# A wait on the landing of the output two windows back, in the scatter queue of a two-layer expert kernel

## The reference, cut to what matters

```python
# layer 1: one expert of 8 for each sequence
h = gelu(x @ Wi[expert] + bi[expert])          # 128 -> 512
o = h @ Wo[expert] + bo[expert]                # 512 -> 128
y = layernorm(o + x) * gamma[expert] + beta[expert]
# layer 2: FiLM on normalised y, then 2 experts of 8 for each token
h = film(time_norm(layernorm(y)))              # gains and shifts from the subject
probs = softmax(h @ router_w)
gates, idx = top_k(probs, 2); gates /= gates.sum()
out = y + sum_k gates[k] * (relu(h @ exp_w1[idx[k]] + exp_b1) @ exp_w2[idx[k]] + exp_b2)
```

## Time and profile before

| what | value |
|---|---|
| timed executions | 211.25, 212.04, 215.63 us; median 212.04 |
| span of the profiled execution | 215.0 us, first to last instruction |
| PE, PEld busy | 172.2 us (80%), 162.9 us (76%) |
| DVE, ACT, POOL busy | 128.2, 94.7, 112.1 us |
| outputs on POOL (L604) | 39, 962 ns each in the mean |

### The profile page before, as it was taken

One profiled execution on the slowest core, in us unless ns is written; L12 is line 12 of the kernel. 1 busy time (PEld: TensorE's weight loads), 2 busy tenths in 40 slices (PEclk: granted clock), 3 DMA queues, 4 the chain that ended last, 5 costly groups with the idle time before them and its releaser, 6 DMA issues.

```text
span 215.0 us, 5253 instructions
## 1 busy us (share of the span) xinstructions
PE 172.2 (80%) x1306; PEld 162.9 (76%) x1306; DVE 128.2 (60%) x635; ACT 94.7 (44%) x311; POOL 112.1 (52%) x168
## 2 busy tenths in 40 slices
PE   7999999999999996799926997436998999987000
PEld 6878999999998986689826896316998999976000
DVE  4515848999989998689725566003345455534154
ACT  2116444677484495537505462024454655552000
POOL 8860012556768987675762307773354454455300
PEclk9999999999999999999995999655799999999655
DMA  3999702999911684586741773211678667252294
GB/s 80 276 303 365 255 0 44 187 287 359 320 48 42 172 244 91 146 204 159 195 148 42 220 200 110 61 49 43 190 197 254 213 197 228 63 175 87 43 391 177
DMA packets 33950, 36.90 MB, mean 172 GB/s; under 512 B 4104, under 2 KB 23376, under 8 KB 33792
## 3 DMA queue, kind: packets, MB, share of 16 engines
q1 hardware_dynamic: 30528, 30.04, 50.3%
q0 software_dynamic: 2912, 6.44, 9.2%
q10 hardware_dynamic: 480, 0.08, 0.2%
HBM read 28.83 MB, written 7.71 MB: 170 GB/s over the span
## 4 chain that ended last, share of the span: by engine, by line
PE 59%; DVE 17%; issue 9%; DMA 5%; another core or an unknown queue 4%; SPq 2%; ACT 1%; DVEq 1%; POOL 1%; ACTq 0%; POOLq 0%
PE bank L1516 15%; PE bank L1501 13%; PE bank L1404 7%; PE bank L1422 6%; PE bank L1315 4%; PE bank L1301 3%; PE bank L1491 3%; DMA o_all<-o_rows 2%; DMA pairs<-pair_rows 2%; DVE st L808 2%; PE bank L1419 2%; DVE y_all L1107 1%; SPq L364 1%; DVE y_all L1106 1%
## 5 line engine op out<-in xcount | busy, mean ns | idle before, releaser
L1207 ACT ACTIVATE hidden<-bank,b_c 128x128 f32<-128x128 f32 x156 | 44.4, 369 | 47.4 <-PE bank L1501 27.0
L604 POOL DMA_INDIRECT o_rows<-weighted,dest x39 | 37.5, 962 | 32.6 <-DVE weighted L967 28.8
L1516 PE MATMUL bank<-w_sb,hidden 128*128 x312 | 45.5, 290 | 5.2 <-issue 3.2
L1501 PE MATMUL bank<-h_t,win_w 128*128 128x128 f32 x312 | 44.4, 288 | 6.3 <-issue 5.0
L1501 PEld LDWEIGHTS bank<-h_t,win_w 128*128 128x128 f32 x312 | 40.6, 202 | 7.5 <-issue 4.5
L1516 PEld LDWEIGHTS bank<-w_sb,hidden 128*128 128x128 f32 x312 | 40.9, 203 | 6.9 <-issue 6.5
L599 POOL DMA_INDIRECT pair_rows<-rows,slot x32 | 32.3, 1010 | 18.9 <-DVE slot L898 8.7
L1147 ACT ACTIVATE hidden<-bank,bi_c 128x128 f32<-128x128 f32 x88 | 24.6, 372 | 14.3 <-PE bank L1404 11.7
L964 DVE TENSOR_TENSOR biased<-bank,b_all 128x128 f32<-128x128 f32 x39 | 11.3, 290 | 32.8 <-PE bank L1516 14.8
L1404 PE MATMUL bank<-x_t,win_w 128*128 (+1 forms) x176 | 25.2, 297 | 0.7 <-DVE x_t L736 0.7
L1404 PEld LDWEIGHTS bank<-x_t,win_w 128*128 128x128 f32 x176 | 23.3, 210 | 1.1 <-issue 1.0
(11 more groups left out here) (228 smaller groups left out, 237.7 us busy)
## 6 DMA issues: line engine op xcount, KB each, us to landing
win_w<-in_L_cond_exp_w_dram SPq DMA_DIRECT2D x39, 256.0 KB
win_w<-in_L_cond_Wi_dram SPq DMA_DIRECT2D x22, 256.0 KB
pairs<-pair_rows SPq DMA_DIRECT2D x39, 65.0 KB
wo_sb<-in_L_cond_Wo_dram SPq DMA_DIRECT2D x8, 256.0 KB, 6.0
w_sb<-in_L_cond_exp_w_dram SPq DMA_DIRECT2D x8, 256.0 KB
o_all<-o_rows SPq DMA_DIRECT2D x4, 512.0 KB, 5.5
y_rows<-y SPq DMA_DIRECT2D x11, 128.0 KB
o_all<-in_x_dram SPq DMA_DIRECT2D x4, 256.0 KB, 5.2
```

The lines of the kernel that those rows point to most:

```text
L604: pool.indirect_dma_start(o_rows, bass.IndirectOffsetOnAxis(dest[:, w:w + 1], 0), weighted[:, w % OUTS, :], None).then_inc(o_stored[w % OU ...
L1207: A.activation(hidden[:, w % 3, ft * P:(ft + 1) * P], bank[w % 2][:, ft * P:(ft + 1) * P], ACT.Relu, bias=b1_flat[:, bass.ds(bias, FT)][:, ...
L1501: last = mm(bank[w % 2][:, ft * P:(ft + 1) * P], win_w[:, (NW + w) % RING, ft * P:(ft + 1) * P], h_t[:, w % 3, :], start=True, stop=True)
L1516: last = mm(bank[3 + w % 2][:, 0:D], hidden[:, w % 3, ft * P:(ft + 1) * P], w2_sb[:, bass.ds(expert, FF)][:, ft * D:(ft + 1) * D], start=( ...
```

## The change: output w waits for output w-2

In `store_out`, from w = 2 on, POOL waits not only for the weighted rows of window w but also until output w-2 has landed. Each of the twelve semaphores gets 16 for every twelfth output, hence the count in the wait.

```diff
             def store_out(w):
                 pool.wait_ge(s["weighted_ready"], w + 1)
+                if w >= 2:
+                    pool.wait_ge(o_stored[(w - 2) % OUTS], 16 * ((w - 2) // OUTS + 1))
                 pool.indirect_dma_start(o_rows, bass.IndirectOffsetOnAxis(dest[:, w:w + 1], 0),
                                         weighted[:, w % OUTS, :], None).then_inc(o_stored[w % OUTS], 16)
```

## The result

The change took 216.17 us (median of 4 executions, 215.37 to 218.85), the kernel before beside it 213.47 (4 executions, 211.25 to 215.63). The ratio is 1.0212, 95% interval [1.0153, 1.0272]. Some executions of either kernel take 1.5% or more longer than its fastest, so a ratio compares only the others, while the medians hold all of them. A second measurement in a later batch gave 215.11 against 211.81, ratio 1.0263 [1.0138, 1.0388]. So the change is slower by 2.1 to 2.6%, 4.5 to 5.5 us, where +0.6 us was predicted. Two traces of the kernel before differ by 6.3 us in their first part alone (DVE's last `slot` row, of block 4, starts at 127.44 and at 121.12), so I align all traces on that row: "from the slot row" means from its start.

What follows compares the result with a forecast made beforehand. PE was taken to hold 59% of the chain of waits, with outputs on it only at the end. Terms 0 + 0 + 0 + 0.6 us on the 212.04 us median gave 212.6 us, range 206.5 to 216.5.

Steps and rivals of the forecast that it cites:

- the freeze: Stretch from 134 to 147 where PE does 18 matmuls in 13 us; forecast to hold until about 147 either way.
- the dense run: POOL's 13 back-to-back scatters from 128.47 to 143.65, one each 1.264 us, beside the PE standstill.
- the run of 4 to 11: Outputs 4 to 11: each pair from 6 on 0.56 us later, output 11 by 1.68; cost taken as nothing.
- A wait that is met: Wait before 37 outputs, already over when reached: cost taken as nothing, or 0.1 us at 0.05 us each.
- A late wait: Landing 2.21 us plus restart 0.88: two outputs need at least 3.09 us, where POOL now takes 2.53.
- my 0.88: Assumed us from landing to the next scatter's start, from a scatter waiting for several semaphores; 0.27 the other end.
- Outputs 12 to 32: Steady outputs, two per 3.80 us: wait over in time at 3.09, pairs 0.7 behind at 4.51; nothing on the path.
- up to three pairs: Lag allowed among outputs 12 to 32, 0.7 us a pair, said to run back before the end.
- rival 2: Lag reaches the end: landings of 3.63 us to output 29, output 38 4 to 5 us late, 216.5 us; chance 0.10.
- The tail: Outputs 33 to 38 behind the gather: output 35 waits for 33's landing, output 38 0.7 us late; 0.6 taken.
- Rival 1: The PE standstill loosens as scatters from output 6 on go from 1.264 to 1.54 us: 205 to 208.5 us; chance 0.24.
- Rival 3: POOL starves in the PE standstill too, outputs 6 to 11 losing 1.5 us each: 219 us; chance 0.05.

Runs made afterwards that it cites:

- those with spacers and waits: The change's waits plus a small POOL operation before outputs: power operation before 4 to 32, 221.27 us; memset there and before earlier scatters, 210.18 us.
- the change with the memset: The change plus a 0.33 us memset on POOL before outputs 13 to 32: 203.1 us against before's 186.85 on the faster chip; 216.46 us on another.
- forced pairs: Kernel before, no landing waits; even outputs 14 to 30 also wait for the next window's weighted rows: 215.87 us, ratio 1.0183.
- the waits with even steps: The change's waits plus a memset before outputs 3 to 32 and some scatters of blocks 3 and 4: 210.18 us, ratio 0.9941 against before.

## Why the prediction was wrong

**The step that failed** is the one that costed outputs at nothing as long as nobody waits for their slot: "Nobody waits for these outputs", and for 12 to 32 "On the path: nothing". In its place the runs showed that outputs act on the other engines by their spacing too: in the change window 32's rows come 3.3 us later than in before, and pairs without any landing wait cost 1.8%. I had the freeze before me and saw the dense run beside it, yet asked only whether the run of 4 to 11 would end sooner. (Of "the four other engines" that stand still from 109 to 113, show three; SP has no column there.) Point by point:

- *A wait that is met:* nothing. Right (waits on w-3, ratio 0.9967).
- *A late wait:* predicted 3.09 us for two outputs, measured 2.97. The restart behind a landing is 0.72 to 0.75 us, nearer to my 0.88 than to 0.27. The Trainium skill's queue for waiting instructions ("Perfetto Trace Analysis", section "DMA Instruction — SWDGE (GPSIMD)") would have left 0.27. It is 0.27 where the weighted rows come last, also with two semaphores to wait for; where the landing comes last the measurement decides against it. So what counts is which of the two is late, not that there are two, as I had it.
- *The run of 4 to 11:* the starts came as worked out (two each 2.97 us), and PE got a little more done (26 matmuls for 18). Window 12's rows are ready at 17.6 instead of 20.4, but those of windows 13 and 15 no earlier, so the gain is given back. Taken as 0; the wait in this range alone costs 1.0% [0.6, 1.5], some 2 us. Where these lie, its trace does not tell: output 38 starts 0.3 us later than in before's first trace and 1.3 us later than in its second.
- *Outputs 12 to 32:* I wrote down that landings of 3.63 us would make each pair 0.7 late, without a reason for "up to three pairs" where rival 2 has fourteen outputs, and took the lag as harmless. For the queue itself that came true: the landings that POOL waited for are of 2.8 to 4.8 us in the two traces of the change, outputs fall up to 3.0 us behind their rows, and output 32 is only 0.27 us behind its own in one trace and 0.56 in the other. What I left out is that late landings make pairs of an even stream, and that the other engines then lose time: windows 18 to 32 take 30.5 us for 27.3 in the first pair of traces. In the second (28.4 for 27.6, within what unchanged kernels differ by) the loss comes at window 33 instead, 4.9 us late.
- *The tail:* the working was right in itself: from output 33 to output 38 I had 10.4 us, the trace has 10.25 (189.31 to 199.56), and output 35 starts 6.0 us after 33 as worked out. The waits in the tail alone cost 0.55% [0.16, 0.94], 1.2 us, for 0.6. What was not foreseen is that output 33 itself starts late: 66.2 us from the slot row instead of 62.9, and 66.3 instead of 62.1 in the second pair of traces. That is the other engines' loss in the step before.
- *Rivals.* Rival 1 had the right mechanism, the density of scatters, but it went by the mean step, and what loosens the freeze is an even one. With 1.57 us it goes, at 5% gain; with 1.98 us it goes too, and POOL becomes the bound. The change's pairs have nearly the same mean (1.54 by the forecast, 1.49 measured), still 1.27 us apart within, and do not do it. The Trainium skill's fetch that is hidden ("Runtime: NRT & Kernel Launch", section "Instruction fetch mechanics") was weighed against that rival; no run shows what the frozen engines wait for, but the runs tie it to scatters all the same. Rival 2 (the lag reaches the end) did not happen where the engines stall, since outputs 32 and 33 have caught up. It is what bounds the kernels whose engines do not stall: those with spacers and waits, and the change with the memset on the faster chip. Rival 3 did not happen: POOL's late waits restart in 0.72 us inside the freeze too.

**What the runs leave.** A landing that is late by more than two steps has two prices, and they are tied. It bunches the outputs, which costs the other engines on chips that stall; and it delays POOL, which costs where PE would otherwise be done first. Shown are forced pairs (1.8%), the waits with even steps (+9.7 us) and the waits on w-3 (nothing). Only argued is that the change's own pairs are what delays window 32 or 33, and how the 4.5 to 5.5 us divide, as the two pairs of traces divide them differently. The 2 us of the early waits have no place in a trace. Open is what stalls the engines, and why one of the chips does not do it.

## What to carry to other kernels

Before adding a wait on a DMA's landing, compare landing under load plus restart with as many steps of the stream as the wait looks back: here two steps (3.8 us) were too few, three (5.7 us) free, for late landings of 3.7 to 4.4 us and a restart of 0.72. Treat back-to-back indirect DMAs as a load on all engines: if PE, DVE and ACT show "issue" gaps while POOL scatters without a pause, space the scatters by a small operation that just keeps POOL ahead (0.33 us here, 5% faster on the chips that stall; not run on the one that doesn't), and look whether the run only moved. A queue with slack because others stall is no queue with slack: cost an edit also for the kernel in which the stall is gone.

## What the runs showed of the hardware

- Scatters of 128 rows, 1.26 to 1.27 us apart, all but stop the instruction streams of the other engines in runs of eight and of thirteen: 18 matmuls in 13 us, and from 135.7 on, when six had gone out, nine in 11.3 us. Behind a shorter run, of three outputs and the gather, the next window's rows came 5.2 us after the last ones. At 1.57 us apart PE does 93 in 13 us, at 1.98 us 119.
- This depends on the chip: in five measurements, on at least four chips, the kernel before took 211.6 to 213.5 us, on one more chip 186.9. Around a run of seven at 1.26 us PE did 118 matmuls in 13 us on that chip and 51 on another, in the same kernel.
- A scatter that waits for a landing and for weighted rows starts 0.72 to 0.75 us after the landing, where this comes last, and 0.27 to 0.28 us after the rows, where they do.
- A scatter of 64 KB lands 2.2 us after its start on quiet queues; under load, where POOL had to wait for it, 2.7 to 4.8. Behind the 1 MB gather it took 5.1 to 7.3 us, and once 3.8.
